# Attention and gated MLP on one core: the attention output through DRAM, divided in the last stage

## The chip, the core and the metric
The kernel runs on 1 core of one Trainium2 chip. The metric is the device time of one execution in microseconds; "before" is the median of 3 runs. Engines: PE (TensorE), DVE (VectorE), ACT (ScalarE), POOL (GpSimd), SP (SyncE, which here only issues DMAs).

## The reference
For x of [2, 1024, 512] (2048 tokens), with 32 heads of 16:

```
xn  = layernorm(x)
q, k, v = split(clip(xn @ Wqkv.T, -8, 8));  q, k = layernorm_w_b(q), layernorm_w_b(k)
p   = softmax_causal(q k^T / 4 + alibi)
s   = (p v) @ Wout.T
g   = silu( (silu(xn @ Wg) * (xn @ Wu)) @ Wd )       # Wg, Wu, Wd from 4-bit integers, zeros, scales; inner size 1792
out = x + s * g
```

## The kernel before
Three blocks of instructions follow one another, each with a program of its own for every engine, and a barrier between them.

**Stage 1 (to about 190 us)** normalises x, projects q, k and v and stores them to DRAM (`stk` for q and k in three bf16 parts, `vscr` for v with a column of ones behind every head, so that P.V gives the softmax's denominator too).

**Stage 2 (about 190 to 764 us), attention.** `groups` runs 16 groups (NG): 2 batches of 8 groups of 4 heads. A group i has 12 steps e (NSTEP). Steps 0 to 7 are the queries 512 to 1023 (k = 0 in `copy_o`), steps 8 to 11 the queries 0 to 511 (k = 1). In a step PE computes transposed scores with the row maximum in them (`second`, L957 to L966), ACT takes the exponential (`exps`, L842), and PE multiplies with V (`pv`, L975) into the one bank `b_o`, of which head j owns rows 32j to 32j+16: 16 rows of O^T and the denominator. After step 7 and after step 11 ACT copies `b_o` to the one tile `ot` (`copy_o`, L849). The first copy is called O1, the second O0; ACT reaches O1 before the exponentials of step 9, and O0 at the group's end, behind which stand, if i is even, two conversions of the MLP's weights (L855, L856), and then the next group's exponentials. `trans_o` (L984) transposes `ot` back in 4 blocks of 128, and DVE's `normalise` (L888, L891) takes reciprocals of the 16 denominators of a partition and multiplies into `o_sb`.

The maxima of the next group are found beside this: PE computes plain score pieces (`score`, L274) into three banks in turn (`b_m`), DVE reduces each (`take`, L264 and L267) and frees the bank. This is the ring: PE may start turn n when DVE has freed turn n - 3 (`m_free`). Which piece stands at which of the 36 places of a group is set by `plan`, with three things in the ring that are no pieces: D0 (the maxima, split in bf16 parts by POOL's `chain`, transposed by PE at L944, copied by DVE at L900), O1 and O0 (the transposes above). The maxima come back into the operands through a small DMA that ACT issues (L827), for which PE waits at the start of a group (`d1_in`) and at step 8 (`d0_in`).

SP's queue holds, per group: a third or two of the MLP's weights (`half_job`, 3 DMAs of 448 KB, after POOL is done with the ones before), then, when `pv` of step 7 is done, the loads of half b = 1 for group i + 2 (14 DMAs, `load`, L176 to L180), and, when step 11 is done, those of half b = 0 (15 with V). The last two groups load nothing.

**Stage 3 (about 764 us to the end)** has 4 blocks of 512 tokens. A block has 14 iterations of 128 inner columns. PE: `gate_up` (24 matmuls, L1318) of the next iteration, then `down` (12 matmuls, L1330) of this one. ACT: silu, the high part of every float32 operand (products are made as three products of high and low parts). DVE: silu times up (L1251), the low part `h_lo` (L1253). POOL: low parts of the weights (L1089). Before the iterations each block has `load_o` (ACT gathers one tile of O from `o_sb`), `trans_o` (PE, L1279), `hi_o`, `lo_o` (high part on ACT, low part on DVE, L1230) and `s_project` (12 matmuls, L1301), four times, through two halves of one bank pair.

Of the kernel before, what the change touches and what calls it, by code (L numbers as in the profile page):

```python
# [5 lines left out]
F32 = mybir.dt.float32  # L25
# [30 lines left out]
def build(nc, x, wproj, lnw, w_all, z_all, s_all, ident_in, identb_in, tri_in, behind_in, qrows, krows, out):  # L56

    stk = nc.dram_tensor("stk", [2, BATCH, P, KT, 3, SEQ], BF16).ap()
    vscr = nc.dram_tensor("vscr", [BATCH, QT, P, GROUPS, GH * VW], F32).ap()

# [3 lines left out]
    with ExitStack() as ctx:  # L64
# [33 lines left out]
        oin = oin_v[:, 0:D]  # L98
# [27 lines left out]
        o_sb = sb("o_sb", [P, NG, QT, GH * HD], F32)  # L126
        with ExitStack() as cb:
# [13 lines left out]
            rec = sbb("rec", [P, 2, 4, GH], F32)  # L141
        with ExitStack() as cc:
# [10 lines left out]
            xnc = sc("xnc", [P, 2, D], F32)  # L153

# [60 lines left out]
        D0_AT, D1_AT, O1_AT = 5, 10, 9  # L215
# [17 lines left out]
        plan[3 * O1_AT + 2].append("O1")  # L233
        tail = LATE[HEAD - TAIL:HEAD] + ["O0"]

        own = [x for h in range(PLACES) for x in plan[h] if x in LATE[HEAD:] or isinstance(x, str)] + ["O0"]
        order = [x for h in range(PLACES) for x in plan[h]] + tail
        RING = len(order)
# [3 lines left out]
        number = ({x: n for n, x in enumerate(order)}, {x: n for n, x in enumerate(own)})  # L242
# [467 lines left out]
        ot_done, rec_done, o_clear = sem("ot_done"), sem("rec_done"), sem("o_clear")  # L710
# [7 lines left out]
        PV0 = 3  # L718

# [4 lines left out]
        def full_d1(i):  # L724

            return USES[0] * i + D1_USE + 2

# [8 lines left out]
        with nc.Block() as block:  # L736
            @block.sync
            def _(sp):
# [9 lines left out]
                sp.dma_start(behind[:, :], behind_in).then_inc(mask_in, 16)  # L748
                for b in (1, 0):
                    load(sp, 1, 1, b)  # L750
                half_job(0)

                def body(i, s, ip, last):
                    if s == 1:
                        half_job(3 * ip + 2)
                    if not last:
                        half_job(3 * ip + (1, 3)[s])
                    else:

                        sp.wait_ge(pv_done, PV0 + NSTEP * i)  # L760
                        for u in range(4):
                            load_x(sp, 0, u)
                    if last is None:
# [3 lines left out]
                        load(sp, i + 2, s, 1)  # L767

                        sp.wait_ge(pv_done, PV0 + NSTEP * i + NSTEP)
                        apart(sp, "sp")  # L770
                        load(sp, i + 2, s, 0)
                groups(sp, body)

            @block.gpsimd
            def _(pool):
                pool.sem_inc(ot_done, EXTRA)
                pool.sem_inc(pv_done, PV0)

# [45 lines left out]
            def _(act):  # L824
# [57 lines left out]
            def _(dve):  # L882
                def normalise(i, k, last):

                    work, qb = ("O1", "O0")[k], 1 - k
                    dve.wait_ge(m_full, base(i) + at(work, last) + 1)
                    src = ring_bank(work, last)[:, :].rearrange("p (t j w) -> p t j w", t=4, j=GH)
                    dve.reciprocal(rec[:, k, :, :], src[:, :, :, HD]).then_inc(rec_done, 1)  # L888
                    dve.wait_ge(rec_done, 2 * i + k + 1)
                    dst = o_sb[:, bass.ds(i, 1), 4 * qb:4 * qb + 4, :].rearrange("p a t (j d) -> p (a t) j d", j=GH)  # L890
                    dve.tensor_tensor(dst, src[:, :, :, 0:HD], rec[:, k, :, :].unsqueeze(3).to_broadcast([P, 4, GH, HD]),  # L891
                                      ALU.mult).then_inc(m_free, 1)

                def ring(i, work, last=None):

                    for x in work:
                        if x == "D0":
                            dve.wait_ge(m_full, base(i) + at(x, last) + 1)
                            apart(dve, "dve")
                            dve.tensor_copy(dt_sb[0][:, :], ring_bank(x, last)[0:48, 0:P // 2].bitcast(BF16)).then_inc(m_free, 1)  # L900
                        elif isinstance(x, str):
                            normalise(i, int(x == "O0"), last)
# [22 lines left out]
            def _(pe):  # L925
                def ring(i, s, work, last=None):

                    for x in work:
                        if isinstance(x, str):
                            pe.wait_ge(m_free, base(i) + at(x, last) - 2)  # L930
                            if x == "D0":
                                trans_d(2 * i + 1, ring_bank(x, last), m_full)
                            else:
# [498 lines left out]
```

## Time and profile before

| what | us |
|---|---|
| runs | 1293.94, 1298.67, 1304.78 |
| median | 1298.67 |
| profiled execution: span, first to last instruction | 1300.7 |
| PE busy | 1205.7 |
| DVE busy | 754.4 |
| ACT busy | 626.0 |
| POOL busy | 503.3 |

The profile gives no time of the profiled execution but its span. It lies within the range of the runs, so sums are made against the span. Busy times of matmuls overlap at their ends.

### The profile page before, as it was taken

How to read it: one execution, taken by the hardware profiler on the slowest of the kernel's cores; microseconds unless marked ns; L12 is line 12 of the kernel's file. 1: busy time of each engine (PE TensorE's matmuls, PEld its weight loads, DVE VectorE, ACT ScalarE, POOL GpSimd, SP SyncE). 2: the span in 40 equal slices, each digit the busy share in tenths (PEclk: the TensorE clock that was granted, in tenths of full speed). 3: DMA queues.
4: the chain of work that ended last, by engine and by line, in shares of the span. 5: the costliest groups of instructions: out<-in, count | busy, mean ns of one | idle time of the engine just before them, and what ended most of it. 6: DMA issues, size and time to landing. Idle time of an engine off the chain costs nothing. (4 is left out here: it accounts for less than half of the span.)

```text
span 1300.7 us, 23572 instructions
## 1 busy us (share of the span) xinstructions
PE 1205.7 (93%) x6848; PEld 768.9 (59%) x6848; DVE 754.4 (58%) x1835; ACT 626.0 (48%) x955; POOL 503.3 (39%) x544
## 2 busy tenths in 40 slices
PE   6999987999999899899998989999999999999997
PEld 5777752333333333333333358887888888888886
DVE  6877887877877778778777622225222522252223
ACT  3333332666666566566665764335433443344332
POOL 2755550313131221212131333555455445545553
PEclk9999986999999999999999989999999999999999
DMA  6234454454546444555565210001100010011000
GB/s 222 91 115 131 138 163 133 116 144 105 147 105 143 99 118 84 125 107 149 107 149 108 83 69 1 1 1 40 57 0 0 32 65 0 0 33 65 1 1 33
DMA packets 101901, 106.62 MB, mean 82 GB/s; under 512 B 28385, under 2 KB 81121, under 8 KB 101729
## 3 DMA queue, kind: packets, MB, share of 16 engines
q1 hardware_dynamic: 75392, 93.10, 27.7%
q10 hardware_dynamic: 26464, 12.98, 3.4%
q8 instruction: 22, 0.36, 0.1%
q14 instruction: 23, 0.18, 0.0%
HBM read 84.41 MB, written 21.23 MB: 81 GB/s over the span
## 5 line engine op out<-in xcount | busy, mean ns | idle before, releaser
L842 ACT ACTIVATE pr<-pair 128x1024 f32<-128x1024 f32 (+3 forms) x384 | 293.6, 811 | 179.7 <-PE pair L965 101.3
L1089 POOL TENSOR_TENSOR ws_lo<-w_f,ws_hi 128x512 fp32r<-128x512 f32 x168 | 238.0, 1445 | 271.8 <-ACT ws_hi L1130 271.8
L264 DVE CUSTOM_DVE_ANT_0 bank<-bank,sg 128x384 f32<-128x384 f32 (+3 forms) x512 | 242.3, 515 | 97.7 <-PE bank L274 94.4
L1251 DVE TENSOR_TENSOR sg<-pair,sg 128x512 f32<-128x512 f32 x56 | 38.8, 692 | 276.0 <-ACT sg L1188 276.0
L1318 PE MATMUL pair<-xc_hi,ws_lo 128*128 128x512 f32 x448 | 175.4, 392 | 0.0
L1318 PE MATMUL pair<-xc_lo,ws_hi 128*128 128x512 f32 x448 | 175.2, 391 | 0.0
L1318 PE MATMUL pair<-xc_hi,ws_hi 128*128 128x512 f32 x448 | 175.1, 391 | 0.0
L267 DVE TENSOR_REDUCE mx<-bank 128x1 f32<-128x512 f32 x256 | 159.8, 683 | 7.4 <-PE bank L274 6.7
L1188 ACT ACTIVATE sg<-pair 128x512 f32<-128x512 f32 x56 | 33.5, 598 | 235.7 <-PE pair L1318 235.6
L799 POOL TENSOR_TENSOR w_f<-w_f,zst 128x896 f32 (+1 forms) x24 | 50.1, 2088 | 215.2 <-ACT zst L856 215.2
L274 PE MATMUL bank<-xin_c,s_sb 108*128 108x512 bf16 (+3 forms) x384 | 118.3, 354 | 13.1 <-DVE mx L264 10.2
L274 PE MATMUL bank<-ks,qs 108*128 108x512 bf16 (+3 forms) x384 | 111.6, 337 | 7.9 <-DVE mx L264 6.9
L1130 ACT ACTIVATE ws_hi<-w_f 128x512 fp32r<-128x512 f32 x168 | 99.1, 627 | 30.2 <-PE bank L1330 28.4
L960 PE MATMUL pair<-qs,ks 111*128 111x512 bf16 (+3 forms) x384 | 97.1, 338 | 16.2 <-DMA qs<-dt 10.4
L960 PE MATMUL pair<-s_sb,xin_c 111*128 111x512 bf16 (+3 forms) x384 | 97.5, 339 | 14.9 <-DMA s_sb<-dt 10.6
L1253 DVE TENSOR_TENSOR h_lo<-sg,h_hi 128x512 fp32r<-128x512 f32 x56 | 71.1, 1271 | 47.7 <-ACT h_hi L1130 47.7
L1318 PEld LDWEIGHTS pair<-xc_hi,ws_hi 128*128 128x128 f32 x448 | 84.6, 189 | 17.7
L1318 PEld LDWEIGHTS pair<-xc_hi,ws_lo 128*128 128x128 f32 x448 | 84.6, 189 | 17.5
L1318 PEld LDWEIGHTS pair<-xc_lo,ws_hi 128*128 128x128 f32 x448 | 84.4, 188 | 17.5
L274 PEld LDWEIGHTS bank<-xin_c,s_sb 108*128 108x128 bf16 x384 | 34.3, 100 | 93.8 <-DVE mx L264 52.2
L1330 PE MATMUL bank<-ws_hi,h_lo 128*128 128x512 f32 x224 | 88.0, 393 | 0.4 <-DVE h_lo L1253 0.2
L1330 PE MATMUL bank<-ws_hi,h_hi 128*128 128x512 f32 x224 | 87.3, 390 | 0.0
(101 smaller groups left out, 1980.0 us busy)
## 6 DMA issues: line engine op xcount, KB each, us to landing
stk<-parts ACTq DMA_DIRECT2D x16, 768.0 KB, 5.9
zst<-in_z_all SPq DMA_DIRECT2D x24, 448.0 KB, 4.2
sst<-in_s_all SPq DMA_DIRECT2D x24, 448.0 KB, 5.0
w_f<-in_w_all SPq DMA_DIRECT2D x24, 448.0 KB, 6.8
xin_c<-in_x SPq DMA_DIRECT2D x32, 256.0 KB, 2.7
s_sb<-stk SPq DMA_DIRECT2D x96, 64.0 KB
xin_c<-stk SPq DMA_DIRECT2D x96, 64.0 KB
qs<-stk SPq DMA_DIRECT2D x96, 64.0 KB
```

The lines of the kernel that those rows point to most:

```text
L264: dve.tensor_tensor_reduce(out=src, in0=src, in1=tri[:, 512 - w:512], scale=1.0, scalar=-3.0e38, op0=ALU.add, op1=ALU.max, accum_out=dst). ...
L267: dve.tensor_reduce(dst, src, AX.X, ALU.max).then_inc(m_free, 1)
L274: pe.matmul(b[:, 0:w], qs[s][0:ROWS_MAX, qt // 4, j, (qt % 4) * P:(qt % 4 + 1) * P], ks[s][0:ROWS_MAX, j, k0:k0 + w], start=True, stop=Tru ...
L799: pool.tensor_tensor(w, w, zst[:, :], ALU.subtract).then_inc(z_sub, 1)
L842: act.activation(pr[e % 3][:, 2 * p:2 * p + 2, 0:w], pair[p][:, :, 0:w], ACT.Exp, scale=SCALE)\
L960: mm = pe.matmul(pair[p][:, jj, 0:512 - c0], ks[s][0:ROWS, j, kt * P:(kt + 1) * P], qs[s][0:ROWS, qb, j, c0:512], start=True, stop=not dia ...
L1089: return pool.tensor_tensor(dst, src, hi.bitcast(F32), ALU.subtract)
L1130: return act.activation(dst, src, ACT.Copy)
L1251: dve.tensor_tensor(sg[s][:, :], pair[s][:, 1, :], sg[s][:, :], ALU.mult).then_inc(h_mul, 1)
L1253: dve.tensor_tensor(h_lo[s][:, :], sg[s][:, :], h_hi[s][:, :].bitcast(F32), ALU.subtract).then_inc(hl_done, 1)
L1318: mm = pe.matmul(pair[s][:, g, :], l, r, start=(k == 0 and n == 0), stop=(k == KT - 1 and n == 2))
L1330: mm = pe.matmul(y[t][:, :], l, r, start=(it == 0 and n == 0), stop=(it == IT - 1 and n == 2))
```

## The change
- `copy_o` stays, but nothing transposes `ot` any more. SP stores it whole (256 KB) to a DRAM tensor `oscr`, after O1 and after O0. Since there is one `ot`, every copy waits until the store before it has landed (`ot_out`).
- In SP's queue the store of O1 stands behind the loads of b = 1, the store of O0 behind those of b = 0. In the last group SP also issues the loads of stage 3's first block, 16 DMAs and 2 MB. Stage 2 ends only when all stores have landed.
- O1, O0, `trans_o`, `normalise` and `o_sb` go. The ring had 51 turns a group, a multiple of 3; to keep that with 49 things in it, D0 counts as three turns: the piece behind D0 uses D0's bank, and waits until DVE has copied D0.
- In stage 3 the tiles `num_c` and `den_c` (4 x 512 float32 a partition each) are loaded from `oscr` per block: O^T as it is, the denominator's row sent to each of the 16 rows of its head. DVE divides (`divide`: a reciprocal of 128x512 and a multiply, 4 times a block), ACT takes the high parts (`hi_o`), DVE the low ones (`lo_o`), both now for the whole block. For block 0 this stands before the iterations, behind the split of x; for blocks 1 to 3 in iterations 4 to 9 of the block before. `s_project` waits once for all four low parts.

```
+            def load_on(sp, b):
+                for n, g in enumerate(range(GROUPS)):
+                    rows = slice((g % 2) * 64, (g % 2) * 64 + 64)
+                    src = oscr[bass.ds(b, 1), g, :, :].rearrange("a (j r) s -> (a j) r s", j=GH)
+                    sp.dma_start(num_c[rows, g // 2, :], src[:, 0:HD, :]).then_inc(on_in, 16)
+                    sp.dma_start(den_c[rows, g // 2, :], src[:, HD:HD + 1, :].to_broadcast([GH, HD, 512])).then_inc(on_in, 16)
@@ plan
-        plan[3 * O1_AT + 2].append("O1")
-        tail = LATE[HEAD - TAIL:HEAD] + ["O0"]
+        tail = LATE[HEAD - TAIL:HEAD]
-        RING = len(order)
+        RING = len(order) - 1 + D0_TURNS
@@ sync, attention
+                def store_o(i, k):
+                    sp.wait_ge(ot_done, EXTRA + 2 * i + k + 1)
+                    apart(sp, "sp")
+                    dst = oscr[bass.ds(2 * (i // GROUPS) + 1 - k, 1), bass.ds(i % GROUPS, 1), :, :]
+                    sp.dma_start(dst.rearrange("a b p s -> (a b p) s"), ot[:, :]).then_inc(ot_out, 16)
...
                         load(sp, i + 2, s, 1)
+                    store_o(i, 0)
+                    if last is None:
                         sp.wait_ge(pv_done, PV0 + NSTEP * i + NSTEP)
                         apart(sp, "sp")
                         load(sp, i + 2, s, 0)
+                    store_o(i, 1)
                 groups(sp, body)
+                sp.wait_ge(ot_out, OT0 + 16 * 2 * NG)
@@ scalar, copy_o
                     act.wait_ge(pv_done, PV0 + NSTEP * i + (FIRST, NSTEP)[k])
+                    act.wait_ge(ot_out, OT0 + 16 * (2 * i + k))
                     act.activation(ot[:, :], b_o[:, :], ACT.Copy).then_inc(ot_done, 1)
@@ vector, D0
-                            dve.wait_ge(m_full, base(i) + at(x, last) + 1)
+                            dve.wait_ge(m_full, base(i) + at(x, last) + D0_TURNS)
-                            dve.tensor_copy(dt_sb[0][:, :], ring_bank(x, last)[0:48, 0:P // 2].bitcast(BF16)).then_inc(m_free, 1)
+                            dve.tensor_copy(dt_sb[0][:, :], ring_bank(x, last)[0:48, 0:P // 2].bitcast(BF16)).then_inc(m_free, D0_TURNS)
@@ vector, last stage
+                def divide(b, k):
+                    if k == 0:
+                        dve.wait_ge(on_in, ON * (b + 1))
+                    dve.reciprocal(den_c[:, k, :], den_c[:, k, :]).then_inc(o_rec, 1)
+                    dve.wait_ge(o_rec, KT * b + k + 1)
+                    dve.tensor_tensor(num_c[:, k, :], num_c[:, k, :], den_c[:, k, :], ALU.mult).then_inc(o_div, 1)
...
+                        if ON_AT <= it < ON_AT + KT and not last:
+                            divide(b + 1, it - ON_AT)
+                        if ON_AT + 2 <= it < ON_AT + 2 + KT and not last:
+                            lo_o(b + 1, it - ON_AT - 2)
@@ tensor, last stage
-                    trans_o(b, 0)
                     gate_up(b, 0)
-                    trans_o(b, 1)
-                    s_project(b, 0)
...
+                    for u in range(4):
+                        s_project(b, u)
```

How the instructions stand, on SP between the two loads of a group. Before, the last issues of b = 1 and the first of b = 0 (`s_sb` and `xin_c` hold q and k of an even group):

```order
L178 DMA s_sb<-in_qrows 12x4x512
L180 ISA
L180 DMA xin_c<-in_krows 15x4x512
L769 REGISTER_ALU
L176 REGISTER_ALU [waits pv_done]
L176 DMA s_sb<-stk 16x4x512
```

Now:

```order
L161 DMA s_sb<-in_qrows 12x4x512
L163 ISA
L163 DMA xin_c<-in_krows 15x4x512
L746 ISA
L749 ISA [waits ot_done]
L749 ISA
L749 DMA oscr<-ot 128x512
L775 REGISTER_ALU
L159 REGISTER_ALU [waits pv_done]
L159 DMA s_sb<-stk 16x4x512
```

The store of O1 stands between the two, behind all 14 DMAs of b = 1.

On DVE, one of the iterations 6 and 7 of a block of the last stage. Before (`sg` is the gate's silu, `pair` the up product):

```order
L1250 REGISTER_ALU
L1251 TENSOR_TENSOR sg<-pair,sg 128x512 [waits silu_done]
L1253 TENSOR_TENSOR h_lo<-sg,h_hi 128x512 [waits hh_done]
L1250 REGISTER_ALU
L1251 TENSOR_TENSOR sg<-pair,sg 128x512 [waits silu_done]
```

Now:

```order
L1246 TENSOR_TENSOR sg<-pair,sg 128x512 [waits silu_done]
L1248 TENSOR_TENSOR h_lo<-sg,h_hi 128x512 [waits hh_done]
L1217 RECIPROCAL den_c<-den_c 128x512
L1218 REGISTER_ALU
L1219 TENSOR_TENSOR num_c<-num_c,den_c 128x512 [waits o_rec]
L1223 TENSOR_TENSOR oc_lo<-num_c,oc_hi 128x512 [waits o_hi]
L1245 REGISTER_ALU
L1246 TENSOR_TENSOR sg<-pair,sg 128x512 [waits silu_done]
```

A divide and a low part of the next block stand between an iteration's `h_lo` and the next iteration's multiply.

## Rows read from the trace of the kernel before

**Rows 1.** The page's busy times: us (share of the span) xinstructions.

```profile
PE 1205.7 (93%) x6848; PEld 768.9 (59%) x6848; DVE 754.4 (58%) x1835; ACT 626.0 (48%) x955; POOL 503.3 (39%) x544
```

**Rows 2.** Timeline of ACT, groups 0, 7, 13: start, us, what [idle].

```profile
248.43 0.94 ACT L856 ACTIVATE zst<-zst 128x896 f32<-128x896 int32 x1
...
249.27 3.75 ACT L842 ACTIVATE pr<-pair 128x1024 f32<-128x1024 f32 x4
...
489.87 0.60 ACT L849 ACTIVATE ot<-bank 128x512 f32<-128x512 f32 x1 [1.10 <-PE bank L975]
...
492.84 1.02 ACT L842 ACTIVATE pr<-pair 128x1024 f32<-128x1024 f32 x1 [2.37 <-PE pair L960]
...
703.29 2.05 ACT L842 ACTIVATE pr<-pair 128x1024 f32<-128x1024 f32 x2 [3.47 <-PE pair L960]
```

**Rows 3.** Timeline of SP: last load of b=1, groups 0, 7, 13.

```profile
248.28 0.87 SPq L180 DMA_DIRECT2D xin_c<-in_krows  x1
...
490.52 0.88 SPq L180 DMA_DIRECT2D ks<-in_krows  x1
...
699.85 0.88 SPq L180 DMA_DIRECT2D ks<-in_krows  x1
```

**Rows 4.** Timeline of PE, start of group 9.

```profile
529.20 0.74 PE L960 MATMUL pair<-qs,ks 111*128 111x512 bf16 x2 [3.06 <-DMA qs<-dt]
```

**Rows 5.** DMA issues: xcount, KB each, median us to landing; x's loads apart.

```profile
vscr<-vst SPq DMA_DIRECT2D x16, 272.0 KB, 3.2
...
out<-s_sb SPq DMA_DIRECT2D x16, 256.0 KB, 2.0
...
DMA to landing us min/median/max: 2.4/2.7/7.5
```

**Rows 6.** Windows: PE, PEld, DVE, ACT, POOL busy (x), PEclk, DMA share, GB/s.

```profile
491.00:492.00 1.00, 0.37 (x3) 0.11 (x2) 0.73 (x4) 0.00 (x0) 0.00 (x0) 0.99 0.89 127
492.00:493.00 1.00, 1.00 (x4) 0.45 (x3) 0.03 (x1) 0.16 (x1) 0.00 (x0) 0.50 0.79 141
```

**Rows 7.** Timeline of PE: the piece behind D0, group 7.

```profile
476.22 0.39 PE L274 MATMUL bank<-xin_c,s_sb 108*128 108x512 bf16 x1
```

**Rows 8.** Timeline of DVE: the copy of D0, group 7.

```profile
476.68 0.21 DVE L900 COPY dt<-bank 48x128 bf16<-48x128 bf16 x1
```

**Rows 9.** Groups by shape: xcount | busy, mean ns | idle before, releaser.

```profile
L888 DVE RECIPROCAL rec<-bank 128x16 f32<-128x16 f32 x32 | 8.2, 258 | 22.5 <-PE bank L984 20.6
...
L280 DVE TENSOR_TENSOR mx<-mx 128x16 f32<-128x16 f32 x16 | 2.8, 175 | 0.6
...
L1251 DVE TENSOR_TENSOR sg<-pair,sg 128x512 f32<-128x512 f32 x56 | 38.8, 692 | 276.0 <-ACT sg L1188 276.0
...
L1253 DVE TENSOR_TENSOR h_lo<-sg,h_hi 128x512 fp32r<-128x512 f32 x56 | 71.1, 1271 | 47.7 <-ACT h_hi L1130 47.7
...
L1330 PE MATMUL bank<-ws_hi,h_lo 128*128 128x512 f32 x224 | 88.0, 393 | 0.4 <-DVE h_lo L1253 0.2
...
L984 PE MATMUL bank<-ident,ot 128*128 128x128 f32 x128 | 20.9, 286 | 5.7 <-ACT ot L849 5.7
```

**Rows 10.** Chain of waits, last stage: start, us, what.

```profile
770.40 0.69 DVE xc_lo L1236
...
779.39 2.77 PE bank L1301 x12
...
881.49 5.44 PE pair L1318 x24
```

**Rows 11.** Timeline of PE, start of block 1 of the last stage.

```profile
902.78 0.38 PE L1279 MATMUL pair<-ident,oin_v 128*128 128x128 f32 x2
...
922.11 0.40 PE L1318 MATMUL pair<-xc_hi,ws_lo 128*128 128x512 f32 x1
```

**Rows 12.** Timeline of ACT, change of stage.

```profile
762.06 0.60 ACT L849 ACTIVATE ot<-bank 128x512 f32<-128x512 f32 x1 [0.53 <-PE bank L975]
...
764.49 0.63 ACT L1130 ACTIVATE ws_hi<-w_f 128x512 fp32r<-128x512 f32 x1 [1.84 <-PEq L736]
```

More of the change, by code:

```diff
@@ L232, in build @@
         plan[3 * D0_AT + 2].append("D0")
-        plan[3 * O1_AT + 2].append("O1")
-        tail = LATE[HEAD - TAIL:HEAD] + ["O0"]
-        own = [x for h in range(PLACES) for x in plan[h] if x in LATE[HEAD:] or isinstance(x, str)] + ["O0"]
+        tail = LATE[HEAD - TAIL:HEAD]
+        own = [x for h in range(PLACES) for x in plan[h] if x in LATE[HEAD:] or isinstance(x, str)]
         order = [x for h in range(PLACES) for x in plan[h]] + tail
-        RING = len(order)
+        RING = len(order) - 1 + D0_TURNS
         assert RING % 3 == 0
@@ L241, in build, with numbered @@
         PREP = len(HEAD_ORDER)
-        number = ({x: n for n, x in enumerate(order)}, {x: n for n, x in enumerate(own)})
+        def numbered(work):
+            return {x: n + (D0_TURNS - 1 if "D0" in work[:n] else 0) for n, x in enumerate(work)}
+        number = (numbered(order), numbered(own))
         def at(x, last):
@@ L718, in build @@
         PV0 = 3
+        OT0 = 16
         def full(i, e, p, last):
@@ L882, in _ @@
             def _(dve):
[L883 to L892, printed above, removed]
                 def ring(i, work, last=None):
@@ L938, in ring, with trans_d @@
                             score(pe, 1 - s, x, ring_bank(x, last), base(i) + at(x, last))
-                def trans_d(n, to, done):
+                def trans_d(n, to, done, turns=1):
                     pe.wait_ge(d_chain, 5 * n + 5)
@@ L944, in trans_d @@
                     pe.transpose(to[0:48, 0:P // 2].bitcast(BF16), d3[:, :, :].rearrange("p a b -> p (a b)"), identb[:, :])\
-                      .then_inc(done, 1)
+                      .then_inc(done, turns)
                 def slot0_free(i, e, last):
@@ L978, in pv @@
                     mm.then_inc(pv_done, 1)
-                def trans_o(i, k, to):
-                    pe.wait_ge(ot_done, EXTRA + 2 * i + k + 1)
-                    for t in range(4):
-                        mm = pe.transpose(to[:, t * P:(t + 1) * P], ot[:, t * P:(t + 1) * P], ident[:, :])
-                    mm.then_inc(m_full, 1)
                 for n in range(len(EARLY), PREP):
@@ L1060, in body @@
                 def body(b, last):
+                    if not last:
+                        sp.wait_ge(o_lo, KT * (b + 1))
+                        apart(sp, "sp")
+                        load_on(sp, b + 1)
                     for u in range(4):
@@ L1197, in body @@
                         copy(h_hi[it % 2][:, :], sg[it % 2][:, :]).then_inc(hh_done, 1)
+                        if ON_AT < it <= ON_AT + KT and not last:
+                            hi_o(b + 1, it - ON_AT - 1)
                         if it + 1 < IT:
@@ L1242, in _ @@
                     lo_x(0, u)
+                for k in range(KT):
+                    divide(0, k)
+                for k in range(KT):
+                    lo_o(0, k)
                 def body(b, last):
-                    for u in range(4):
-                        lo_o(b, u)
                     for it in range(IT):
@@ L1270, in _ @@
             def _(pe):
-                def trans_o(b, u):
-                    if u == 0:
-                        pe.wait_ge(xc_l, 4 * b + 4)
-                    pe.wait_ge(o_in, 4 * b + u + 1)
-                    if u > 1:
-                        pe.wait_ge(o_lo, 4 * b + u - 1)
-                    for k in range(KT):
-                        mm = pe.transpose(pair[1][:, u % 2, k * P:(k + 1) * P], oin[:, k * P:(k + 1) * P], ident[:, :])
-                    mm.then_inc(o_tr, 1)
                 def trans_x(b, u):
```

82 lines of the change are left out of this document (34 added, 48 removed).

## The prediction, made before the kernel ran
> **What bounds the kernel now.** I read the page first: PE is busy for 93% of the span, so the end is set by PE's work and by what holds it up [rows 1]. The timelines of one group of the attention stage come next, since the change puts a wait there. ACT copies the finished O0 out of its bank at 489.87 and begins the next group's exponentials at 492.84; between the two only PE's restart holds it [rows 2]. The SP queue in the same stretch: after the eighth P.V step it issues 14 loads for the group after the next, the last until 491.40 (490.52 + 0.88), so it is issuing still when ACT takes O0 [rows 3]. PE's own hold-up at a group's start is the small transfer of the maxima, 3.06 us in the group shown, nothing in others [rows 4]. In the last stage the chain of waits is matmuls end to end: 12 projections 2.77 us, 24 gate-up matmuls 5.44, the 12 of down half of that, 2.72 [rows 10].
>
> **A. The copy of O0 waits for the store of O1 (slower, the largest term).** There is one tile `ot`. SP stores O1 only behind the 14 loads, and the copy of O0 now waits for that store. So the copy starts at (end of the 14 issues) + 0.3 (SP's gap before an issue) + L (issue to landing) + 0.1. It takes 0.6, and where the group's convert stands behind it, in seven of the 14 groups, two conversions of 0.94 come before the exponentials too [rows 2]. Behind the waiting copy stand exactly these: the conversions and the next group's exponentials, and PE cannot pass its second step without the latter. The exponentials then start L + 1.0 after the last issue ends in seven groups, L + 2.9 in the other seven.
> Before, they started this long after it, group by group: 0.12, 0.34, 1.20, 0.90, 1.22, 1.40, 5.43, 1.44, 3.69, 1.66, 1.07, 1.26, 1.75, 2.56 us, 24.0 in all (first: 249.27 less 249.15; eighth: 492.84 less 491.40; last: 703.29 less 700.73 [rows 2, 3]). The last two groups load nothing, so their stores are early.
> L is not in the trace, since nothing is stored from this stage. The nearest row is the 272 KB store of V from the same queue beside other traffic, 3.2 us; the ends are 2.0 (256 KB of output, queue empty) and 7.5 (the slowest 256 KB load of x, queued behind 1.3 MB) [rows 5]. I take 3.2: 7 x 6.1 + 7 x 4.2 - 24.0 = **+48.1**. At 2.0 it is +31.3, at 7.5 +108.
> PE meanwhile does the score pieces of its first step, so some 0.4 us a group comes back (between 0 and 1): **-5.6**. The longer idle time also lets the clock fall: after PE was busy for 0.37 us of a microsecond the granted clock was 0.50, the 1.2 GHz level, in the next one [rows 6]. Some groups show that today, others not; over all of them I add **+6**, from 0 to 20 (it stays low for some 4 us, which can cost 2).
> The Trainium skill ("DMA: Bandwidth & Descriptors", the two cost components) gives 2.0 us fixed plus bytes over 436 GB/s, an estimate of 2.6 us for 256 KB. By it A would be +39.7 in place of +48.1. Our empty-queue store of 2.0 us lies under that figure, the busy one over it.
>
> **B. O1 and O0 no longer pass through PE and DVE (faster, mostly covered).** Eight transposes, two reciprocals and two multiplies go from every group. The transposes were busy for 20.9 us and waited for 5.7 over 16 groups [rows 9], 1.7 us a group; their ends overlap with the next matmuls, so I take 1.3. Both stand behind the eighth P.V step, inside the stretch that A makes longer, so in 14 groups they give nothing. The two groups without loads keep it: **-2.6**. If A were not there it would be -21 (16 x 1.3).
>
> **C. D0 takes three turns of the ring (slower).** The next score piece now waits until DVE has copied D0. PE issued that piece at 476.22 [rows 7]; DVE came to the copy at 476.68 and left it at 476.89, two reductions behind [rows 8]. The piece moves to about 476.97, and DVE gets it about 0.6 us later than it would have begun it, in a stretch where DVE has no idle time to absorb it. It lies ahead of the eighth P.V step, so nothing covers it: 16 x 0.6 = **+10** (0 to 15).
>
> **D. The change of stage (slower).** The last store must land before the stage ends. O0's last copy began at 762.06 and the next stage's first work at 764.49 [rows 12]. Now: store issued at about 763.0, landed 3.2 later, 766.2, less the normalising that goes, and the store of O1 stands in a queue behind 2 MB of loads of the new tiles: **+3** (0 to 7).
>
> **E. First block of the last stage (slower).** Four reciprocals and four multiplies of 128x512 stand between the split of x and the projections, with only the first gate-up beside them. A reciprocal of 16 elements took 258 ns where a 16-element maximum took 175 [rows 9]. Taking the rate of one element per 1.04 ns from the 128x512 multiply (692), the fixed part is 158, which leaves 6.2 ns an element, 3.4 us for 512; with no fixed part at all it is 16 ns, 8.3 us. I take 4.0, near the lower end, since a one-input operation's fixed part may be smaller. Each divide is 4.0 + 0.69 + 0.25 between them, four are 19.8, and four splits 2.8: 22.6. They begin when the split of x ends, 770.40 + 0.69 = 771.1, and end at 793.7. The projections began at 779.39 and, 4 x 2.77 and 0.9 of transposes later, ended at 791.3 [rows 10]; now they start at 793.7 and take 11.1, plus 1.9 at the low clock after 15 us of idle PE: 806.7, **+15.4** (13 to 33).
> The Trainium skill ("VectorE: DVE Perf Modes", the walkthrough of the pipeline) says that reciprocal runs divide steps with a repeat count of 8; at eight passes of 1.04 ns the operation would be an estimate of 4.4 us, and E would be +17.
>
> **F. Later blocks (faster).** From the first transpose of O at 902.78 to the second gate-up at 922.11 pass 19.3 us [rows 11], of which the matmuls that stay are 16.5 (5.44 + 4 x 2.77). The 2.8 left were transposes and the wait for copies and splits: 3 x 2.8 = **-8.4**. The divides of these blocks lie in iterations 4 to 7 of the block before. DVE idles (276.0 + 47.7) / 56 = 5.8 us an iteration [rows 9]; a divide takes 4.0 + 1.27 and two iterations have a split of 1.27 as well, 6.5. The 0.7 over has room: silu, multiply, high part and split take about 4 us after a gate-up ends, while the matmul on h_lo comes 2.72 + 5.44 = 8.2 us after it, and PE waited for it 0.2 us in 224 matmuls [rows 9, 10]. I cost this at **0**; without the cover it is rival 2.
>
> **Sum.** 48.1 - 5.6 + 6 - 2.6 + 10 + 3 + 15.4 - 8.4 = +65.9. The profiled execution's span was 1300.7, so 1366.6. The median of the runs is 2.0 below the span, so the forecast is 1364.6.
>
> **Rivals.**
> 1. Covered store, not slower. ACT could reach O0 no sooner than the store lands, because PE's restart waits for the maxima's transfer. For it: that wait was 3.06 us in the group shown [rows 4], and two of 14 gaps exceed 3.6 us. It decides if L + 1.0 (or + 2.9) is below the gaps, mean 1.7; against it, that takes an L below zero in most groups, or stores that are reached before the loads, which the order denies. Then A is 0 and B is whole: -21 + 10 + 3 + 15.4 - 8.4 = -1, so 1298; with C at its lower end 1288. Chance 0.06.
> 2. DVE becomes the bound of the last stage. If a reciprocal takes 8.3 us, four iterations hold 8.3 + 1.27 + 2.0 + 0.9 = 12.5 us of DVE, and more with the split, where PE needs 8.16. After 4 us of room that is +14 in each of three blocks, with E at +33: 1365 + 42 + 17 = 1424. For it: nothing shows a wide reciprocal. Against it: 158 of the 258 ns look fixed. Chance 0.07.
> 3. The store is slow. It queues behind loads still moving, as the x loads did at 7.5: A +108, so 1425. Its half, L of 5.0, gives 1390. Chance 0.17 for L above 4.6.
> 4. A costs a third. The store lands in 2.0, PE and DVE recover 1 us a group from the pieces done early, and the clock does not fall: A is 31.3 - 14 = 17, the sum 17 - 2.6 + 10 + 3 + 15.4 - 8.4 = +35, so 1333. For it: 1.3 us of PE's work of the first step lies behind no exponential. Against it: two of its conditions are ends of their ranges. Chance 0.15.
>
> My forecast has 0.55. Its own range is 1345 to 1385. The range given, 1328 to 1402, leaves out rival 1, most of rival 2 and the far part of rival 3. Runs of this kernel differ so that 1% is about what can be told from no change. Faster by over 1% has 0.02, within 1% 0.05, slower by over 1% 0.93.
>
> **What would show it.** In the profile after: ACT's copy of `ot` idle before it for 4 to 6 us in every second copy, released by a DMA; PE's first-to-second step gap grown by as much; groups of about 39 us in place of 34.9 (703.29 less 249.27 [rows 2], over 13); one PE gap of 15 us before the first projection; reciprocals near 4 us; no PE gap at the later blocks' starts. It is wrong if the copy of O0 does not wait, if the stores are issued before the loads, or if L lies far from 3.2.

## The result: 1387 us, 6.9% slower

The changed kernel took 1387.43 us (median of 4 runs, 1386.97 to 1389.8), the kernel before 1299.22 beside it on the same chip. The ratio is 1.0685 (95% interval 1.0648 to 1.0722). The direction and the mechanism came as forecast, and the time lies in the range given, but 23 us above the number and 2 us above its own range of 1345 to 1385. The profiled span is 1385.2, that is 84.5 over the 1300.7 of before, where the sum had 65.9.

The page of the changed kernel: span, busy times in the form of [rows 1], and the stores of the attention stage among the DMA issues (KB each, median us to landing), which the kernel before did not have.

```profile
span 1385.2 us, 23318 instructions
...
PE 1211.5 (87%) x6656; PEld 753.2 (54%) x6656; DVE 805.9 (58%) x1803; ACT 618.1 (45%) x939; POOL 507.4 (37%) x544
...
oscr<-ot SPq DMA_DIRECT2D x32, 256.0 KB, 2.9
```

PE has 192 instructions fewer and is busy 6 us longer. So 79 of the 84.5 us are idle time. The transposes that went had been busy for 20.9 us [rows 9], so the work that stays is busy some 27 us longer. The list of waits says where PE and ACT stood (us in total, times, longest):

```profile
PE pair L955 <- ACT pr L852: 51.6, 16, 5.0
...
PE pair L955 <- DMA qs<-dt: 15.8, 8, 3.4
PE pair L955 <- DMA s_sb<-dt: 14.4, 8, 4.4
...
PE bank L1291 <- DVE oc_lo L1223: 11.1, 1, 11.1
PE bank L260 <- DVE dt L900: 10.3, 15, 0.7
...
ACT ot L860 <- DMA oscr<-ot: 91.0, 15, 7.9
```

The last row is term A, the row of `dt L900` term C, and that of `oc_lo` term E. In ACT's timeline, group 7 of the changed kernel answers to the eighth group in [rows 2]:

```profile
528.30 0.66 ACT L852 ACTIVATE pr<-pair 128x256 f32<-128x256 f32 x2 [0.94 <-PE pair L960]
534.26 0.60 ACT L860 ACTIVATE ot<-bank 128x512 f32<-128x512 f32 x1 [5.30 <-DMA oscr<-ot]
534.75 2.85 ACT L852 ACTIVATE pr<-pair 128x1024 f32<-128x1024 f32 x3
```

SP's queue beside it, as in [rows 3]. The last load is issued until 531.61, the store of O1 at 532.16, and ACT's copy of O0 starts 2.10 us after that:

```profile
530.74 0.87 SPq L163 DMA_DIRECT2D ks<-in_krows  x1
532.16 0.39 SPq L749 DMA_DIRECT2D oscr<-ot  x1
```

PE, same place. It does its first step (531.54), waits 2.76 us for the exponentials, and the P.V step at 538.23 then takes 1.86 us (the same eight matmuls took 1.05 us in run e6 below, at 502.96, with the granted clock at 1.00):

```profile
531.54 0.60 PE L955 MATMUL pair<-s_sb,xin_c 111*128 111x512 bf16 x2 [1.15 <-DMA s_sb<-dt]
...
535.83 0.60 PE L955 MATMUL pair<-s_sb,xin_c 111*128 111x512 bf16 x2 [2.76 <-ACT pr L852]
...
538.23 1.86 PE L970 MATMUL bank<-pr,oin_v 128*17 128x512 f32 x8
```

The windows of that stretch show why (columns as in [rows 6]): PE is nearly idle from 533 to 536, and the granted clock is at 0.50, the 1.2 GHz level, from 537 to 539, after which it returns.

```profile
533.00:534.00 1.00, 0.07 (x1) 0.00 (x0) 1.00 (x5) 0.00 (x0) 0.00 (x0) 1.00 0.77 276
534.00:535.00 1.00, 0.00 (x0) 0.00 (x0) 0.16 (x2) 0.74 (x2) 0.00 (x0) 1.00 0.50 127
535.00:536.00 1.00, 0.17 (x1) 0.11 (x2) 0.00 (x0) 1.00 (x2) 0.00 (x0) 1.00 0.46 132
...
537.00:538.00 1.00, 1.00 (x4) 0.15 (x1) 1.00 (x4) 0.70 (x2) 0.00 (x0) 0.50 0.56 138
538.00:539.00 1.00, 1.00 (x5) 0.16 (x8) 0.58 (x3) 0.93 (x1) 0.00 (x0) 0.50 0.47 129
539.00:540.00 1.00, 1.00 (x8) 0.00 (x0) 0.24 (x2) 0.00 (x0) 0.00 (x0) 0.55 0.45 96
```

At the end of group 4 the wait was longer, and so was what followed: the clock stood at 0.50 from 414 until 423. The rows of its third and ninth microsecond:

```profile
416.00:417.00 1.00, 0.00 (x0) 0.00 (x0) 0.00 (x0) 1.00 (x2) 0.03 (x1) 0.50 0.49 130
...
422.00:423.00 1.00, 1.00 (x6) 0.23 (x3) 0.00 (x0) 0.00 (x0) 0.00 (x0) 0.50 0.79 171
```

**Where the 84.5 us are.** I cut ACT's timeline at three events of each group: the copy of O1, the copy of O0, and the first exponential of the next group. Two sums over 14 groups then carry most of it. "Turn" is from the copy of O1 to the next first exponential, and holds the wait of A. "Run" is from the first exponential to the next copy of O1, and holds the work in which D0 stands and in which the clock comes back.

| stretch | before | after | difference |
|---|---|---|---|
| start to the first copy of O1 | 239.8 | 240.4 | +0.7 |
| turn, 14 groups | 149.3 | 182.2 | +32.9 |
| run, 14 groups | 339.3 | 374.2 | +34.9 |
| group 14: turn | 9.5 | 9.0 | -0.5 |
| group 15: run | 18.8 | 22.9 | +4.1 |
| group 15: copy of O1 to copy of O0 | 5.4 | 12.9 | +7.5 |
| last copy to the next stage's first work | 2.4 | 3.2 | +0.7 |
| last stage | 536.2 | 540.4 | +4.2 |

They add up to 84.5. The run was 23.85 us in most groups before and is 26.0 to 27.4 now. Over the 14 runs the granted clock stood at 0.50 for 15 us before and for 81 us now, and every run now has at least 3.4 us of it.

The last stage's first block in the changed kernel: DVE's first division and the split, then PE's first projection, and its projections in the chain of waits.

```profile
851.47 3.34 DVE L1217 RECIPROCAL den_c<-den_c 128x512 f32<-128x512 f32 x1
...
867.42 3.56 DVE L1223 TENSOR_TENSOR oc_lo<-num_c,oc_hi 128x512 fp32r<-128x512 f32 x4
```

```profile
871.11 0.79 PE L1291 MATMUL bank<-wo_hi,oc_lo 128*128 128x512 f32 x1 [11.06 <-DVE oc_lo L1223]
```

```profile
871.11 12.80 PE bank L1291 x48
```

From the stage's start at 844.83 to the end of the projections at 883.91 are 39.1 us; before, 764.49 to 791.3, it was 26.8. E is +12.3. The whole stage is only 4.2 longer, so from the end of these projections to the end of the kernel it is 8.1 shorter (509.4 before, 501.3 now), which is F.

### The profile page after: what moved, and what is told of

It reads as the page before. It is cut to its first block and busy times, and to the rows that moved or that the text cites. A ratio compares the mean times of both kernels' runs of the same rounds, so it can differ in the third digit from the quotient of the medians.

```text
span 1385.2 us, 23318 instructions
## 1 busy us (share of the span) xinstructions
PE 1211.5 (87%) x6656; PEld 753.2 (54%) x6656; DVE 805.9 (58%) x1803; ACT 618.1 (45%) x939; POOL 507.4 (37%) x544
## 5 line engine op out<-in xcount | busy, mean ns | idle before, releaser
L1084 POOL TENSOR_TENSOR ws_lo<-w_f,ws_hi 128x512 fp32r<-128x512 f32 x168 | 241.3, 1463 | 284.6 <-ACT ws_hi L1125 284.6
L253 DVE TENSOR_REDUCE mx<-bank 128x1 f32<-128x512 f32 x256 | 160.0, 684 | 16.1 <-PE bank L260 15.4
L955 PE MATMUL pair<-qs,ks 111*128 111x512 bf16 (+3 forms) x384 | 103.4, 356 | 49.4 <-ACT pr L852 31.0
L260 PE MATMUL bank<-xin_c,s_sb 108*128 108x512 bf16 (+3 forms) x384 | 121.7, 364 | 18.0 <-DVE mx L250 10.3
L955 PE MATMUL pair<-s_sb,xin_c 111*128 111x512 bf16 (+3 forms) x384 | 101.6, 350 | 37.9 <-ACT pr L852 20.6
L260 PE MATMUL bank<-ks,qs 108*128 108x512 bf16 (+3 forms) x384 | 115.6, 347 | 13.4 <-DVE mx L250 6.9
L1125 ACT ACTIVATE ws_hi<-w_f 128x512 fp32r<-128x512 f32 x168 | 99.2, 627 | 24.7 <-PE bank L1319 21.7
L792 POOL TENSOR_SCALAR dneg<-mx 128x16 f32<-128x16 f32 x32 | 8.2, 255 | 233.2 <-DVE mx L250 158.6
```

Source lines behind the costliest of these rows:

```text
L253: dve.tensor_reduce(dst, src, AX.X, ALU.max).then_inc(m_free, 1)
L260: pe.matmul(b[:, 0:w], qs[s][0:ROWS_MAX, qt // 4, j, (qt % 4) * P:(qt % 4 + 1) * P], ks[s][0:ROWS_MAX, j, k0:k0 + w], start=True, stop=Tru ...
L955: mm = pe.matmul(pair[p][:, jj, 0:512 - c0], ks[s][0:ROWS, j, kt * P:(kt + 1) * P], qs[s][0:ROWS, qb, j, c0:512], start=True, stop=not dia ...
L1084: return pool.tensor_tensor(dst, src, hi.bitcast(F32), ALU.subtract)
L1125: return act.activation(dst, src, ACT.Copy)
```

## The experiments

Two theories stood after the profile. The first: the wait of A is made by the order of SP's queue (the store of O1 behind the loads) together with the single tile. The second: a large part of the rest is the low clock behind PE's waits, not the waits. The rivals: the loads or D0's turns set the time.

**e1: two tiles.** No copy waits for the other's store.

```
-            ot = sbb("ot", [P, 512], F32)
+            ot = [sbb(f"ot{n}", [P, 512], F32) for n in range(2)]
...
-                    act.wait_ge(ot_out, OT0 + 16 * (2 * i + k))
+                    act.wait_ge(ot_out[k], OT0 + 16 * i)
```

> The changed kernel with two tiles ot, one for O1 and one for O0, each with a semaphore for its stores, so that the copy of O0 never waits for the store of O1. Theory (the store wait costs twice, once directly, 39 us over 14 groups, and once more because PE comes out of it at the 1.2 GHz level, about 2 us a group): both go, and the removed transposes count in all groups, 1387 - 39 - 28 - 15 = about 1305, at most 1315; first exponential to O1 copy back near 24.6 us a group. Rival (the longer stretch from the first exponential to O1 comes from D0's three turns or from the stores' traffic, not from the wait): that stretch stays at 26.8 and the time is 1387 - 39 - 18 = 1330 or more.

Measured: 1328.7 us (1327.72 to 1333.2), ratio 1.0219 (1.0169 to 1.027). Of 88 us, 59 go with the wait. The turn is 146.2, even below before's 149.3. But 30 us are left, more than theory expected. Cut like the table above, this trace has +22.0 in the runs and +15.1 from group 15 on, less 6.4 in the start and the turns. Of the 15.1, 5.7 stand between the last copy and the next stage's first work, which are 8.1 us apart (2.4 before): the last stores, behind the burst of loads, now hold up the end of the stage in place of the copy of O0. The waits of PE say why the turns gained so little:

```profile
PE pair L958 <- DMA s_sb<-dt: 24.8, 8, 4.9
...
PE pair L958 <- DMA qs<-dt: 16.1, 8, 3.6
```

That is 41 us, where the kernel before waited 21 for the same transfers (8 times 10.6 in total, 6 times 10.4):

```profile
PE pair L960 <- DMA s_sb<-dt: 10.6, 8, 4.0
PE pair L960 <- DMA qs<-dt: 10.4, 6, 4.5
```

So in this kernel B's transposes were cover. They filled PE while the maxima travelled, and with them gone PE stands idle for the same transfer. It also loses its clock there: the run is 361.4 (25.8 a group), with 51 us at the clock of 0.50.

**e8: one tile, the store ahead of the loads.** The single tile stays; only SP's order changes. (The expectation speaks of three or four loads ahead of the store; there are 14 issues.)

```
                         sp.wait_ge(pv_done, PV0 + NSTEP * i + FIRST)
                         apart(sp, "sp")
+                        store_o(i, 0)
                         load(sp, i + 2, s, 1)
-                    store_o(i, 0)
+                    else:
+                        store_o(i, 0)
```

> The kernel after, with the store of O1 issued ahead of the three or four loads that SP has before it in groups 1 to 14, on the same one tile. Theory (the copy of O0 is late because the store stands in SP's queue behind the loads): the store is issued in the roughly 8 us between the copies of O1 and O0 and is out when O0 is ready, the loads go some 1.5 to 2 us later because SP now waits for the copy of O1 first; the wait of the first exponential falls from 63.2 us to about 25 to 35 and the time to 1335 to 1350 us. Rival (the loads bound the stage, so what delays them costs as much): the loads are a further 14 x 2 = 28 us late, time 1360 us or more.

Measured: 1332.22 us (1326.94 to 1334.82), ratio 1.027 (1.0206 to 1.0334). This one move of a line gives 55 us back, and the kernel is within 4 us of e1 (by the ratios within 7). In its group 8 the store is issued at 526.83, the loads follow from 527.65, and the copy of O0 waits for PE, not for a DMA:

```profile
526.83 0.37 SPq L749 DMA_DIRECT2D oscr<-ot  x1
527.65 0.34 SPq L159 DMA_DIRECT2D s_sb<-stk  x1
```

```profile
532.73 0.60 ACT L862 ACTIVATE ot<-bank 128x512 f32<-128x512 f32 x1 [1.19 <-PE bank L972]
```

ACT's waits for the store are 22.2 us in 7 copies, 8.5 of it in group 15, where it is still behind other loads. The rival fell: the b=1 loads are issued later (the last of this group ends at 535.63, after the first exponential at 535.09) and nobody waits for them, since they are for the group after the next.

e8 also says more on B. Its turn is 134.8, which is 14.5 below before's and 11.4 below e1's, though the transposes are gone in both. PE's wait for the maxima is shorter here, 28.5 us in place of e1's 40.9:

```profile
PE pair L957 <- DMA s_sb<-dt: 16.4, 8, 4.0
PE pair L957 <- DMA qs<-dt: 12.1, 8, 3.4
```

At the starts of the groups the transfer took 4.5 us in the mean from its issue to PE's start, in e1 5.3. The loads beside it are issued 1.4 us later in e8, but no run changes that alone, so why the transfer is faster is not shown. Here most of what B took off PE came back as time. What keeps e8 above before is its runs (363.0, so +23.7) and the time from group 15 on (+17.5, of which 7.6 are the late copy of O0).

**e2: D0 with one turn, the last piece of the group with three.** D0's stall goes, and the two spare turns move to a place where PE waits anyway.

```
-        D0_AT, D1_AT, D0_TURNS = 5, 10, 3
+        D0_AT, D1_AT, D0_TURNS, END_TURNS = 5, 10, 1, 3
```

> The changed kernel, but D0 takes one turn of the ring again and the last score piece of a group takes three, where DVE and PE wait for the next group anyway. Theory (the drain at D0 costs 0.75 us a group, the rest of the longer stretch is the low clock after the store wait): 1387 - 12 = 1375, stretch 26.0 us. Rival (the drain at D0 is the whole of the excess, 2.7 us a group): 1387 - 40 = 1347, stretch 24.

Measured: 1388.41 us (1385.19 to 1393.03), ratio 1.0673 (1.0619 to 1.0727), the same as the changed kernel. Both expectations missed. The run fell by 11.0 (374.2 to 363.2), as theory had it, and the turn grew by 16.1 (182.2 to 198.3). Part of that is SP's queue: its next loads stand behind a weight job that waits for GpSimd, so with O1 earlier, the time from O1 to the end of the loads grew by 6.9. The other 9 are the stores: from issue to the copy of O0 they took 3.26 us in the mean of 14, in the changed kernel 2.62. Why they were slower here is not shown. The profiled execution was also this kernel's slowest, 4.6 us above the median.

**e5: the kernel before, with D0 taking four turns.** This measures C by itself.

```
-        D0_AT, D1_AT, O1_AT = 5, 10, 9
+        D0_AT, D1_AT, O1_AT, D0_TURNS = 5, 10, 9, 4
```

> The kernel before with one edit of the change alone: D0 takes four turns of the ring (51 turns become 54), so that the next piece waits for DVE's copy of D0. Theory: 0.75 us a group as the trace after shows at this place, 16 x 0.75 = +12, 1311. Rival 1 (absorbed by DVE's idle time): within 3 us of before. Rival 2 (the drain makes the whole excess of the changed kernel): +30 or more, 1330.

Measured: 1305.35 us (10 runs, one of 1325.39, the others 1299.08 to 1310.79), ratio 1.004 (1.0007 to 1.0073), less than the 1311 expected. The run is 24.52 or 24.53 in 10 groups, where it was 23.85 or 23.86 in 8: the stall costs 0.67, and +5 us are left in the time (+1 to +9 by the interval). The sum of the runs grows by 8.5, and the turn shrinks by 6.1 (149.3 to 143.2). The time from O1 to the end of the loads alone fell by 6.6, about 0.47 a group. C is real and about two thirds covered.

**e3: 16 useless matmuls ahead of step 1.** They keep PE busy while it waits for the exponentials. Their bank is overwritten before anything reads it, so they change no result.

```
+                        if e == 1 and last is None:
...
+                            for _ in range(16):
+                                pe.matmul(ring_bank(x, last)[:, :], qs[s][0:ROWS_MAX, 1, 0, 0:P], ks[s][0:ROWS_MAX, 0, 0:512],
+                                          start=True, stop=True)
```

> The changed kernel with 16 matmuls of 512 columns put before PE's second step of each group but the last two; their result is overwritten by the next score piece and used nowhere. They fill 3.5 us of the wait for the exponentials. Clock theory: PE stays at the 2.4 GHz level, the stretch from the first exponential to O1 falls from 26.8 to about 24.8 us in 13 groups, the time is 1387 - 26 + 3 (the first group, which has little wait) = about 1364. Rival (the clock has no part in it): nothing gained, and up to 5 us lost where the wait is shorter than the filling, 1387 to 1392.

Measured: 1379.1 us (1376.09 to 1387.49), ratio 1.0631 (1.0567 to 1.0696), 8 us less than the changed kernel, a third of what theory wanted. The run falls from 374.2 to 357.3. In groups 1, 5, 9 and 13 it is 24.51 or 24.52, exactly 23.85 + 0.67: full clock and D0's stall. In the others it is 24.7 to 27.7; there PE has already waited for the maxima's transfer, ahead of these matmuls (33.6 us over the stage). The granted clock is at 0.50 for only 9 us of the 14 runs, where it was 81, so the low clock behind the wait is confirmed. What keeps these runs long is mostly the cover: in group 8 its 16 matmuls started at the low clock and ended after the exponentials, and ACT waited 1.56 us for PE.

**e4: e1 with the turns of e2.**

> Two tiles, and the ring's two spare turns moved from D0 to the last piece of a group. Theory (PE waits at the start of a group for the maxima that the ring's last pieces write, not for D0's copy, so only D0's stall of 0.67 us a group goes): first exponential to copy of O1 from about 25.7 to about 25.0 a group, that is 15 x 0.67 = 10 us less, 1318 to 1323 us. Rival (as with the one tile, the stall is covered by the loads' wait for GpSimd's job): 1326 to 1330 us, no change from two tiles alone.

Measured: 1326.23 us (1324.89 to 1331.2), ratio 1.0221 (1.0164 to 1.0278), 2.5 us under e1, but measured beside another set of runs of the kernel before, and the ratios are the same. The rival held: the run is 357.1 in place of 361.4, not 10 less.

**e6: e4 with ten useless matmuls ahead of the wait for the maxima.** They go to the bank that the group's first score piece overwrites.

```
+                        if e == 0 and not last:
+                            x = next(x for h in range(PLACES) for x in plan[h])
+                            pe.wait_ge(m_free, base(i) + at(x, last) - 2)
+                            for _ in range(10):
```

> The kernel with two tiles and end turns, and 10 matmuls of 512 columns without a use ahead of PE's wait for the maxima's DMA at the start of each group but the last, in a bank that is overwritten before it is read. Theory (the wait itself is covered, its cost is the low clock behind it): granted clock 0.99 in the first 8 us of the groups, first exponential to copy of O1 23.9 to 24.5 in all groups, 1305 to 1312 us. Rival (the wait, not the clock, is the cost, or the useless matmuls end later than the DMA lands): no gain, or up to 2 us a group lost, 1325 to 1350 us.

Measured: 1325.91 us (1324.57 to 1326.45), ratio 1.022 (1.0163 to 1.0276): no gain, although the clock came as theory said. The run is 23.85 in most groups, 336.2 in all, 20.9 less than e4. The turn is 163.9, 18.8 more. In these runs the granted clock never stands at 0.50. PE's timeline shows the price: the ten wait 0.86 us for a bank, and then take 3.99 us, most of it at the low clock themselves.

```profile
495.65 3.99 PE L990 MATMUL bank<-xin_c,s_sb 108*128 108x512 bf16 x10 [0.86 <-DVE mx L250]
499.43 0.67 PE L958 MATMUL pair<-s_sb,xin_c 111*128 111x512 bf16 x2
```

**e9: the ten into a bank that is free.** This kernel also has e7's edits (next). The useless matmuls write the second half of `pair[1]`, so they start without a wait.

```
-                            x = next(x for h in range(PLACES) for x in plan[h])
-                            pe.wait_ge(m_free, base(i) + at(x, last) - 2)
                             for _ in range(10):
-                                pe.matmul(ring_bank(x, last)[:, :], qs[s][0:ROWS_MAX, 1, 0, 0:P], ks[s][0:ROWS_MAX, 0, 0:512],
+                                pe.matmul(pair[1][:, 1, 0:512], qs[s][0:ROWS_MAX, 1, 0, 0:P], ks[s][0:ROWS_MAX, 0, 0:512],
```

> The kernel e7 with its ten useless matmuls put into the second half of pair[1], free since the last exponential, in place of a ring bank for which PE waits 0.86 us first. Theory (in e6 and e7 the ten matmuls ran at half the clock, 3.99 us, because PE had waited before them, and ended 1 to 1.8 us after the maxima's DMA was in): they start 0.86 us sooner and partly at full clock, so the first exponential comes about 1.5 us a group sooner, 13 groups, 1310 less 15 to 20 = 1290 to 1295 us. Rival (the first exponential waits for the DMA, not for these matmuls): 1305 to 1311 us.

Measured: 1300.97 us (1296.76 to 1303.48, 10 runs), ratio 0.9998 (0.9967 to 1.003). It is 9 us less than e7, where theory had 15 to 20. Nine of the ten now take 2.10 us, at full clock, and the group's first step follows without a wait:

```profile
523.74 2.10 PE L1003 MATMUL pair<-ks,qs 108*128 108x512 bf16 x9
525.95 0.61 PE L973 MATMUL pair<-qs,ks 111*128 111x512 bf16 x2
```

The turn is 145.4 (e7: 163.4), the run 348.8 (e7: 339.4). Most of what the run has over 14 x 23.85 = 333.9 is in two groups: 30.19 in group 14 (below), and 28.05 in group 1, whose cause I did not look for.

**e7: e6, with the first block's O^T loaded and divided in the attention stage.** The 16 loads go to the start of group 14, one division into the eighth place of group 15's ring, three behind its last piece.

```
+                    if last is False:
+                        for n in range(2):
+                            sp.wait_ge(ot_out[n], OT0 + 16 * GROUPS)
+                        load_on(sp, 0)
...
+                        if last and h == OWN_END:
+                            divide(dve, 0, 0)
...
+                    if last:
+                        for k in range(1, KT):
+                            divide(dve, 0, k)
```

> The kernel before this one, and the loads of the first block's O^T and denominators a group earlier (group 14), its four divisions moved into group 15 (one at its eighth place, three behind the last piece of the ring). Theory: the first projection no longer waits for four reciprocals and multiplies (4 x 4.0 = 16 us of VectorE, of which some 9 to 12 are in PE's wait), and the last copy of O0 no longer stands behind the loads (5 to 7 us): about 1290 us, below the kernel before. Rival (the loads and the divisions only move their delay into groups 14 and 15, whose ring VectorE serves): 1302 to 1315 us.

Measured: 1310.19 us (1306.79 to 1313.31, 10 runs), ratio 1.0082 (1.0053 to 1.0111): 16 us less than e6, 20 more than I wanted. The last stage starts and runs better (the last copy of O0 to the end takes 530.5 us; in e6, 550.7). Group 14 gives some of it back: its run is 27.85 and its turn 13.6, where the others have 23.85 and 11.7 in the mean.

**e10: the loads spread over groups 10 to 13, four each.** Otherwise e9.

> The kernel e9 with the sixteen loads of the first block's O^T and denominators spread, four each behind the last store of groups 10 to 13, in place of all sixteen in group 14. Theory (the burst of 16 in group 14 holds up the two maxima transfers there, 27.85 in place of 23.85 us to the copy of O1, 13.6 in place of 9.0 us to the next first exponential): 6 to 8 us less than e9, 1283 to 1288 us. Rival (four loads in each of four groups hold up a transfer of each by 1 to 2 us): the same as e9 within 2 us.

Measured: 1303.0 us (1298.19 to 1310.89, 10 runs), ratio 1.0006 (0.9966 to 1.0046), the rival: no difference to e9. Group 14's stretches are whole (23.85 and 9.01), but groups 11 and 13 lose what it gained. Their runs are 30.12 and 30.71, because SP's weight job stands behind the four loads and ACT's conversion of its tile stands in front of D0's transfer:

```profile
619.89 0.95 ACT L884 ACTIVATE w_f<-w_f  x1 [4.58 <-DMA w_f<-in_w_all]
620.27 0.72 ACTq L855 DMA_DIRECT2D qs<-dt  x1
```

**e11: the 16 loads behind the last store of group 14.** Otherwise e9.

> The kernel e9 with the sixteen loads of the first block's O^T and denominators behind the last store of group 14 in SP's queue, in place of at the group's start. Theory (in e9 the burst lies over the transfer of D0's maxima, for which PE waits 4.17 us at low clock after, and delays the rest of the group: first exponential to copy of O1 30.19 where 23.85 is the rule, copy of O1 to the next first exponential 12.8 where it is 9.0): the group comes back to 24 and 9 to 10, 9 us less, of which VectorE's first reciprocal, waiting for the loads in group 15, takes 2 to 4 back: 1293 to 1297 us, 0.4 to 0.7% below the kernel before. Rival (the burst holds up D1's or the next D0's transfer instead, or the divisions reach into the first projection): 1299 to 1304 us.

Measured: 1310.32 us (1304.75 to 1320.18, 12 runs), ratio 1.0068 (1.0034 to 1.0103), worse than either expectation. Group 14 is mended as theory said (23.84 and 9.01), but group 15's run is 37.84. DVE's first reciprocal waited 21.17 us for the loads, and ACT's conversion 17.68 for its weights behind them; D0's transfer stands behind the latter in ACT's queue.

```profile
764.11 3.35 DVE L707 RECIPROCAL den_c<-den_c 128x512 f32<-128x512 f32 x1 [21.17 <-DMA den_c<-oscr]
```

```profile
767.45 0.95 ACT L879 ACTIVATE w_f<-w_f 128x896 f32<-128x896 int32 x1 [17.68 <-DMA w_f<-in_w_all]
768.34 0.72 ACTq L850 DMA_DIRECT2D qs<-dt  x1
```

Group 14, groups 10 to 13, the end of group 14: three places for the 2 MB of loads and three times a queue that something else needed. The best version of the changed design, e9, ties with the kernel before. Nothing that ran beats it.

## Why the prediction was right, and what was mis-sized

**A, the wait for the store: right, 48.1 forecast, 39.2 measured.** I compare as the forecast did, by the time from the end of the last load's issue to the first exponential: 24.0 before, 63.2 after. The cause is shown by e1 and e8, each of which takes it away in another way. The forecast's L of 3.2 was the term that was too large for this execution. From the store's issue to the copy of O0 it was 2.10 to 3.42 us, 2.62 in the mean of 14, against 3.3; SP's gap before the issue was 0.55, against 0.3. The copy took 0.5 and copy with conversions 2.2, where I had 0.6 and 2.5. The Trainium skill ("DMA: Bandwidth & Descriptors", the two cost components) led to an estimate of 2.6 us and +39.7 for A, and the measured 39.2 fits it. Part of that is luck. The page fits its figures to DMAs that GpSimd issues, and SP issues these. The same mean of 14 is 2.92 in e3 and 3.26 in e2, where A would be 43.4 and 48.3. And all 32 stores of the changed kernel landed after 2.9 us in the median, between 2.0 and 10.4.

**The low clock and the catch-up: the step that failed.** "Over all of them I add +6", less 5.6 that would come back, came to nearly nothing. The runs grew by 34.9, of which D0's stall is 14 x 0.67 = 9.4 at most. The remaining 25.5, 1.8 us a group, are PE's work at the 1.2 GHz level: e3 brings four groups to 24.51, and e6, where both waits are gone or covered, nearly all to 23.85. The granted clock says the same in five kernels. Take from the 14 runs their floor, 23.85 us each or 24.52 where D0 stalls: what is left is 5.4 us before, 30.9 in the changed kernel, 18.1 in e1, 29.3 in e2 and 4.5 in e5, beside 15, 81, 51, 80 and 12 us at the clock of 0.50. That is 0.36 to 0.38 us lost for each. In e4 and e8 it is 0.5, so something else is in their runs as well. I had set the price per occurrence right ("which can cost 2") and then spread it as if only some groups had it. In the changed kernel the wait stands in every group, and so does the low clock. The 5.6 of catch-up has no place of its own in these numbers. The sum "O1 to end of loads" fell by 6.1, but in e5, without any A, it fell by 6.6, so it belongs to C.

**B, the removed transposes: -2.6 forecast, -0.5 measured.** Group 14 gained 0.5 us and group 15 nothing. "If A were not there it would be -21" was wrong too. In e1 the turn is only 3.1 us below before's, and the waits for the maxima's transfer rose from 21.0 to 40.9, which is about the transposes' 20.9 of [rows 9]. In e8 it is 14.5 below, with 28.5 of such waits. So how much of B is time depends on when the transfer lands. The arithmetic of rival 1 (1298 if A costs nothing) fails with it: with A gone the kernel takes 1329 to 1332, and 1301 only when useless work takes the transposes' place and the first divisions move.

**C, D0's three turns: 10 forecast.** The stall is 0.67 a group by e5 and its profile, close to my 0.6. "Nothing covers it" was wrong: the loads behind it wait for GpSimd's job anyway. +5 was left in e5, and between e1 and e4 the ratios show nothing.

**D, the change of stage: 3 forecast, 12.3 measured.** I priced only the landing of the last store. Of the measured 12.3, 4.1 is the run of group 15, where PE waits for D0's transfer beside the burst of loads and then works at the low clock. Another 7.5 is the copy of O0, which waited 7.95 us:

```profile
825.50 1.03 PE L955 MATMUL pair<-qs,ks 111*128 111x512 bf16 x2 [3.45 <-DMA qs<-dt]
...
841.68 0.60 ACT L860 ACTIVATE ot<-bank 128x512 f32<-128x512 f32 x1 [7.95 <-DMA oscr<-ot]
```

The last 0.7 is the change of stage itself. The text had the ingredient ("the store of O1 stands in a queue behind 2 MB of loads") but gave it no price. A second tile does not remove this cost: in e1 the copy of O0 is in time, and the change of stage takes 5.7 us more. Both are short (4.9 and 3.2 us) only where the burst stands ahead of group 15, in e7, e9, e10 and e11.

**E and F: right.** E 15.4 forecast and 12.3 measured, F -8.4 and -8.1. The reciprocal took 3.34 us, the lower end (3.4) of my bounds, so the fixed part of the 16-element row was indeed fixed:

```profile
L1217 DVE RECIPROCAL den_c<-den_c 128x512 f32<-128x512 f32 x16 | 53.5, 3342 | 0.0
```

It is 6.2 to 6.5 ns an element. The Trainium skill ("VectorE: DVE Perf Modes", the walkthrough of the pipeline) with its repeat count of 8 led to an estimate of 4.4 us, and the measurement decides against that. DVE was not overloaded in the later blocks: PE's wait for h_lo stayed at 0.2 us in 224 matmuls, so rival 2 fell.

**The whole.** A was 9 too high, D 9 too low, E 3 too high, and the clock with D0 and the catch-up 18 too low (28.8, the 34.9 less the 6.1 by which O1 to the end of the loads fell, where I had 10.4). The other 3 us are in the start, B and F. So the range held by luck: its upper part was there for half of rival 3, a slow store (1390), and what filled it was the low clock and the change of stage.

## What to carry to other kernels

When a copy is made to wait for a store, look first at where the store stands in its queue: here moving it ahead of loads that nobody was waiting for gave 55 of 88 us, almost as much as a second buffer. Count each new wait of PE twice, once for its length and once for the work behind it if the clock falls (here 0.36 to 0.38 us for each microsecond at 0.50), and in every group that has it. Work that you take off PE ahead of a wait for a small transfer may be cover and not time (e1 kept 3 us of it, e8 14); ask what PE would be waiting for instead. And before moving a burst of loads, list every store, every small transfer and every conversion behind it: three places for the same 2 MB each hit another.

## What was new of the hardware

From the issue of a 256 KB store beside other traffic to the start of the copy that waited for it, 2.1 to 3.4 us passed in different groups of one execution, with the same code around it, and in e2 up to 4.4. Ten matmuls of 512 columns without a use took 3.99 us in e6, where PE had waited 0.86 us and less just before, and nine took 2.10 in e9, where it had not. In e6 the wait of 0.86 us stood behind stretches in which PE was not fully busy either (0.56 and 0.79 us of the two microseconds ahead of it), and the granted clock was at 0.50 from 497 to 499, in the middle of the ten. In e9 it stayed at 1.00.
